# A decoder layer's expert phase: transposes in 64-row halves, rows turned one tile further ahead

## The chip, the cores and the metric

The kernel runs on one core of one Trainium2 chip. The time is the device time of the whole program in microseconds, the median of three runs. The profile is one further execution, recorded by the hardware profiler.

## The reference

One post-norm decoder layer on x of 128 sequences x 128 tokens x 256 features, all in fp32: causal self-attention (16 heads of 64), cross-attention (16 heads of 16, key mask), and two groups of 32 experts, each with top-2 routing. The change lies in the experts alone. For one group:

```python
order = jnp.argsort(flat_e)
tok = flat_t[order]
xs = x2[tok]
gate = lax.ragged_dot(xs, wg, group_sizes)
up = lax.ragged_dot(xs, wu, group_sizes)
ys = lax.ragged_dot(jax.nn.silu(gate) * up, wd, group_sizes)
ys = ys * flat_w[order][:, None]
return jnp.zeros_like(x2).at[tok].add(ys)
```

There are 16384 tokens, so 32768 rows in each group; an expert's weights are 256x128 (gate, up) and 128x256 (down).

## The kernel before, in words

The program has an attention phase (to about 3400 us) that also routes the tokens and scatters their rows, sorted by expert, to HBM (`xs_d`), and an expert phase. The change is in the expert phase (L1251 to L1532). It works through 576 tiles of 128 rows, each of one expert, 288 for each group; all weights stay in SBUF (`moe`), and TensorE finds the tile's expert by a word of a table that it reads once in four tiles (`find_weights`, L1381, the load on L1397).

Each engine runs its own queue of instructions in program order; semaphores order them among each other. All queues are written by the same loop over iterations n, in which an engine works on several tiles at different stages: `t.live(lag)` and `t.item(lag)` stand for tile n - lag. On TensorE one iteration is: transpose of tile n's rows (L1411, two of 128x128, from `xg` into the bank pair `XB`, one bank per tile in turn); gate and up of tile n-1 (L1419, two matmuls of 256 columns, each of which the chip runs as two passes); finding the weights; transpose of tile n-2's hidden activation h (L1430, one of 128x128 into `HB`); down product of tile n-3 (L1435, one matmul, two passes).

ScalarE copies the transposed rows (L1447) and the transposed h (L1451) from PSUM to SBUF and computes SiLU (L1455), in the order rows n, h of n-2, SiLU of n-1. VectorE multiplies by up (L1496), copies y (L1508) and combines finished rows of tokens; GpSimd writes y to HBM by token (L1366). SyncE loads rows into ten buffers ahead (L1331). TensorE waits for the rows' load, for ScalarE's copy of an earlier tile before it overwrites a bank, and for ScalarE's copies before it uses them.

A transpose on TensorE is a weight load of the data (here 128 columns wide) and a pass of the identity matrix over it. The attention phase uses other tilings of the array too: scores in 64-row halves (L779, pairs into two banks), cross scores in 32-row quarters (L792), and products in 32-column strips (L835, L851); all else works on 128x128.

Of the kernel before, what the change touches and what calls it, by code (L numbers as in the profile page):

```python
# [20 lines left out]
F32 = mybir.dt.float32  # L21
# [8 lines left out]
P = 128  # L30
D = 256
KC = D // P
# [62 lines left out]
def wait(eng, sem, value):  # L95

    if isinstance(value, int) and value <= 0:
        return
    eng.wait_ge(sem, value)
# [67 lines left out]
def decoder_layer(nc, xT, x, cT, mask, wq, wk, wv, wo, xwq, xbq, xwk, xbk, xwv, xbv, xwo, xbo,  # L167
# [4 lines left out]
    NT = NGRP * TILES  # L172
# [10 lines left out]
    keep = ExitStack()  # L183
    with keep:
        def tile(stack, name, shape, dt=F32):
            return stack.enter_context(nc.sbuf_tensor(name, shape, dt))
# [1 line left out]
        def sem(name):  # L188
            return keep.enter_context(nc.semaphore(name))

        banks = [keep.enter_context(nc.psum_tensor(f"bank{i}", [P, 512], F32)) for i in range(8)]


        ident = tile(keep, "ident", [P, P])
# [40 lines left out]
        with ExitStack() as one:  # L235
            def sb(name, shape, dt=F32):
                return tile(one, name, shape, dt)
# [66 lines left out]
            HALVES = (slice(0, P // 2), slice(P // 2, P))  # L304
# [946 lines left out]
        with ExitStack() as two:  # L1251
            def sb(name, shape, dt=F32):
# [6 lines left out]
            NQ, NX, NTO, NR, NS = 4, 10, 8, 4, 8  # L1259
# [14 lines left out]
            xg_s = [sb(f"xg{q}", [P, D + 2]) for q in range(NX)]  # L1274
            to = sb("to", [P, NTO], I32)
            xgT = [sb(f"xgT{q}", [P, KC, P]) for q in (0, 1)]
            gate_s = [sb(f"gate{q}", [P, HID]) for q in (0, 1)]
            h_s = [sb(f"h{q}", [P, HID]) for q in (0, 1)]
            hT_s = [sb(f"hT{q}", [P, P]) for q in (0, 1)]
# [1 line left out]
            stat, mv2 = sb("stat", [P, 6]), sb("mv2", [P, NR, 2])  # L1281
            ve, rstd = sb("ve", [P, NR]), sb("rstd", [P, NR])
            half1 = sb("half1", [P, 1])
            XB, GB, HB, YB = banks[0:2], banks[2:4], banks[4], banks[5:7]

            tabs_ready, pack_step, spare_ready, to_made = (
                sem(n) for n in ("tabs_ready", "pack_step", "spare_ready", "to_made"))
            xg_in = [sem(f"xg_in{q}") for q in range(NX)]
            xgt_made, xgt_in, gu_made, gate_in, h_in, ht_made, ht_in, y_made, y_in = (
                sem(n) for n in ("xgt_made", "xgt_in", "gu_made", "gate_in", "h_in", "ht_made", "ht_in", "y_made", "y_in"))  # L1290
# [27 lines left out]
            with nc.Block() as block:  # L1318
# [53 lines left out]
                @block.tensor  # L1372
                def _(pe):
                    pe.wait_ge(tabs_ready, 1)

                    word, next_word, at_place = (pe.alloc_register(n) for n in ("word", "next_word", "at_place"))
                    columns = [pe.alloc_register(f"column{q}") for q in range(NQ)]
                    loads = [pe.alloc_register(f"load{q}") for q in range(NQ)]
                    pe.reg_load(next_word, tabs[0:1, 0:1])

                    def find_weights(t, group):  # L1381

                        q = t.slot(0)
                        if t.p == 0:
                            pe.reg_mov(word, next_word)
                        pe.reg_alu(at_place, word, q * PLACE_BITS, ALU.logical_shift_right)
                        pe.reg_alu(at_place, at_place, 2 ** PLACE_BITS - 1, ALU.bitwise_and)
                        pe.reg_alu(columns[q], at_place, WCOL, ALU.mult)
                        pe.reg_alu(at_place, at_place, CHUNK.bit_length() - 1, ALU.logical_shift_right)
                        if group:  # L1390
                            pe.reg_alu(at_place, at_place, 4, ALU.add)
                        pe.reg_alu(at_place, at_place, (6, 7)[group], ALU.bitwise_and)
                        pe.reg_alu(at_place, at_place, (2, 5)[group], ALU.add)
                        pe.reg_alu(at_place, at_place, CHUNK_LOAD, ALU.mult)
                        pe.reg_alu(loads[q], at_place, 2 * CHUNK_LOAD, ALU.max)
                        if t.p == 2 and t.u + 1 < NT // PACK:
                            pe.reg_load(next_word, tabs[0:1, bass.ds(t.u + 1, 1)])  # L1397

                    def column(q):
                        return pe.snap(columns[q], min_val=0, max_val=(PLACES - 1) * WCOL)  # L1400

                    def iteration(t, n):

                        if t.live(1):
                            gate_up, load = column(t.slot(1)), pe.snap(loads[t.slot(1)], min_val=0, max_val=9 * CHUNK_LOAD)
                        if t.live(0):
                            q = t.slot(0)
                            pe.wait_ge(xg_in[n % NX], (n // NX + 1) * 16)
                            wait(pe, xgt_in, t.item(1))
                            for k in range(KC):  # L1410
                                last = nc.tensor.transpose(XB[q % 2][:, k * P:(k + 1) * P], xg_s[n % NX][:, k * P:(k + 1) * P], ident[:, :])  # L1411
                            last.then_inc(xgt_made, 1)
                        if t.live(1):
                            q = t.slot(1)
                            pe.wait_ge(moe_in, load)
                            pe.wait_ge(xgt_in, t.item(1) + 1)
                            wait(pe, h_in, t.item(2))
                            for k in range(KC):
                                last = nc.tensor.matmul(GB[q % 2][:, 0:2 * HID], xgT[q % 2][:, k, :],  # L1419
                                                        moe_cols[:, bass.ds(gate_up + k * 2 * HID, 2 * HID)], start=(k == 0), stop=(k == KC - 1))  # L1420
                            last.then_inc(gu_made, 1)
                        if t.live(3):
                            down = pe.snap(column(t.slot(3)) + KC * 2 * HID)
                        if t.live(0):
                            find_weights(t, int(n >= TILES))
                        if t.live(2):
                            q = t.slot(2)
                            pe.wait_ge(h_in, t.item(2) + 1)
                            wait(pe, ht_in, t.item(2))
                            nc.tensor.transpose(HB[:, 0:P], h_s[q % 2][:, :], ident[:, :]).then_inc(ht_made, 1)  # L1430
                        if t.live(3):
                            q = t.slot(3)
                            pe.wait_ge(ht_in, t.item(3) + 1)
                            wait(pe, y_in, t.item(4))
                            nc.tensor.matmul(YB[q % 2][:, 0:D], hT_s[q % 2][:, :], moe_cols[:, bass.ds(down, D)],  # L1435
                                             start=True, stop=True).then_inc(y_made, 1)

                    tiles(iteration)

                @block.scalar  # L1440
                def _(act):
                    def iteration(t, n):
                        if t.live(0):
                            q = t.slot(0)
                            act.wait_ge(xgt_made, t.item(0) + 1)
                            wait(act, gu_made, t.item(1))
                            nc.scalar.copy(xgT[q % 2][:, :, :].rearrange("p k t -> p (k t)"), XB[q % 2][:, 0:D]).then_inc(xgt_in, 1)  # L1447
                        if t.live(2):
                            q = t.slot(2)
                            act.wait_ge(ht_made, t.item(2) + 1)  # L1450
                            nc.scalar.copy(hT_s[q % 2][:, :], HB[:, 0:P]).then_inc(ht_in, 1)  # L1451
                        if t.live(1):
                            q = t.slot(1)
                            act.wait_ge(gu_made, t.item(1) + 1)
                            nc.scalar.activation(gate_s[q % 2][:, :], GB[q % 2][:, 0:HID], ACT.Silu).then_inc(gate_in, 1)  # L1455
                        now = combined(n)
                        if now:
                            g, b, k = now
                            wait(act, stored[k % NS], k // NS * 16)
                            act.dma_start(sums[k % NS][:, :], (x2_d, acc_d)[g][b * P:(b + 1) * P, :]).then_inc(sums_in[k % NS], 16)  # L1460
                            wait(act, sum_ready, k - NR + 1)
                            for q in range(NQ):
                                act.wait_ge(y_out[q], 16 * -(-(g * TILES + tiles_with(b) - q) // NQ))
                            act.dma_start(rows[:, k % NR, :, :].rearrange("p j d -> p (j d)"),
                                          y_of_token[b * P:(b + 1) * P, g * TOPK * D:(g + 1) * TOPK * D]).then_inc(rows_in[k % NR], 16)

                    tiles(iteration)
# [113 lines left out]
```

## Time and profile before

| what | value |
|---|---|
| median of 3 runs | 4448.16 us (4447.42 to 4455.27) |
| profiled execution | 4455.09 us |
| its span | 4453.3 us |
| TensorE busy over the span | 4345.7 us (98%) |
| TensorE weight loads | 3811.3 us (86%) |
| VectorE | 3593.6 us (81%) |
| ScalarE | 3260.3 us (73%) |
| GpSimd | 2715.9 us (61%) |

The busy share is over both phases. PE is TensorE's passes, PEld its weight loads, which run beside the passes; a pass's end is modelled, so the step between the starts of two passes says more than the duration of one. In the chain of work that ended last, followed back from the end, the four TensorE lines of the expert phase come first (L1419 10%, L1435 5%, L1411 3%, L1430 2% of the span).

### The profile page before, as it was taken

To read this page: it belongs to the slowest core of one execution; us is meant where nothing else is said; L and a number is where in the kernel's file an instruction comes from. 1 tells how busy PE (TensorE), PEld (TensorE's weight loads), DVE (VectorE), ACT (ScalarE), POOL (GpSimd) and SP (SyncE) were. 2 spreads that over 40 slices of the span, in tenths; PEclk is the share of its full clock that TensorE was granted. 3 is DMA by queue.
4 is the path that set the end of the run, shared out by engine and by line. 5 is a ranking of instruction groups with operands and counts; after the bars stand their busy time and mean duration, and the time that the engine had idled before them with its cause. 6 is when DMAs were issued, how large, how long until landed. Compare 5 with 4: busy or idle time off the path is not lost. (4 is left out here: it accounts for less than half of the span.)

```text
span 4453.3 us, 137987 instructions
## 1 busy us (share of the span) xinstructions
PE 4345.7 (98%) x42944; PEld 3811.3 (86%) x42944; DVE 3593.6 (81%) x18057; ACT 3260.3 (73%) x12741; POOL 2715.9 (61%) x3747
## 2 busy tenths in 40 slices
PE   8999999999999999999999999999995999999998
PEld 7888888989898989888988898999883778878886
DVE  4888888888888888888888888888885466658888
ACT  6888888888888888888888888888883444444444
POOL 3466566666666665666566656665665555557777
PEclk9999999999999999999999999999996999999999
DMA  5122212112212121122121212222115799988998
GB/s 171 57 68 67 69 63 69 66 63 72 69 66 69 65 68 66 65 72 68 66 70 65 67 66 67 71 68 71 63 62 172 219 342 338 311 276 288 310 310 292
DMA packets 477454, 552.60 MB, mean 124 GB/s; under 512 B 55633, under 2 KB 408145, under 8 KB 476241
## 3 DMA queue, kind: packets, MB, share of 16 engines
q1 hardware_dynamic: 350800, 296.21, 20.8%
q0 software_dynamic: 52224, 146.87, 8.7%
q10 hardware_dynamic: 73728, 100.70, 7.3%
q8 instruction: 376, 6.16, 0.6%
q14 instruction: 326, 2.66, 0.2%
HBM read 266.21 MB, written 277.35 MB: 122 GB/s over the span
## 5 line engine op out<-in xcount | busy, mean ns | idle before, releaser
L902 ACT ACTIVATE prob<-prob,negmax 128x128 f32<-128x128 f32 x2048 | 796.8, 392 | 258.3 <-DVE negmax L1038 258.3
L902 ACT ACTIVATE xprob<-xprob,xnegmax 128x128 f32<-128x128 f32 x2048 | 798.4, 399 | 3.6 <-DVE xnegmax L1038 3.6
L1366 POOL DMA_INDIRECT y_d<-y,to x576 | 562.9, 977 | 354.1 <-DVE y L1508 271.8
L1038 DVE CUSTOM_DVE_ANT_0 prob<-bank,causal 128x128 f32<-128x128 f32 x2048 | 453.8, 286 | 339.5 <-PE bank L792 322.6
L641 POOL DMA_INDIRECT xs_d<-xrow,place x512 | 551.8, 1078 | 139.2 <-issue 139.2
L1419 PE MATMUL bank<-moe,xgT 128*128 x2304 | 595.8, 381 | 1.3 <-issue 1.1
L604 POOL TENSOR_TENSOR rs<-spread_v,minus_half 128x1 f32<-128x1 f32 x256 | 170.9, 668 | 594.5 <-DVE spread_v L1112 591.7
L587 POOL CAST yTh<-yT 128x512 fp32r<-128x512 f32 x256 | 221.2, 864 | 461.3 <-ACT yT L938 461.3
L1038 DVE CUSTOM_DVE_ANT_0 xprob<-bank,xmask 128x128 f32<-128x128 f32 x2048 | 451.9, 287 | 0.5 <-PE bank L792 0.5
L1086 DVE TENSOR_TENSOR xprob<-xprob,xinv 128x512 f32<-128x512 f32 x512 | 438.0, 856 | 17.6
L690 PE MATMUL bank<-xT0h,wqkv 128*128 128x256 f32 x2048 | 436.3, 297 | 12.8 <-DVE wqkv L436 11.4
L690 PE MATMUL bank<-xT1h,wqkv 128*128 128x256 f32 x2048 | 435.5, 296 | 0.0
L1419 PEld LDWEIGHTS bank<-moe,xgT 128*128 128x128 f32 x2304 | 393.8, 191 | 34.1 <-issue 3.9
L902 ACT ACTIVATION_READ_ACCUMULATOR xprob<-xprob,xnegmax 128x1 f32 x2048 | 403.1, 197 | 0.0
L1447 ACT COPY xgT<-bank 128x256 f32<-128x256 f32 x576 | 214.5, 372 | 248.9 <-DMA y_d<-y,to 81.3
L902 ACT ACTIVATION_READ_ACCUMULATOR prob<-prob,negmax 128x1 f32 x2048 | 385.8, 188 | 0.0
L690 PEld LDWEIGHTS bank<-xT0h,wqkv 128*128 128x128 f32 x2048 | 333.3, 189 | 55.7 <-issue 40.8
L1075 DVE TENSOR_TENSOR prob<-prob,inv 128x512 f32<-128x512 f32 x512 | 358.2, 700 | 17.6
L690 PEld LDWEIGHTS bank<-xT1h,wqkv 128*128 128x128 f32 x2048 | 331.7, 188 | 43.2 <-issue 41.1
L1451 ACT COPY hT<-bank 128x128 f32<-128x128 f32 x576 | 152.9, 265 | 293.4 <-PE bank L1430 221.8
L1435 PE MATMUL bank<-moe,hT 128*128 x1152 | 359.0, 393 | 0.3
L589 POOL TENSOR_TENSOR yTl<-yT,yTh 128x512 fp32r<-128x512 f32 x256 | 328.7, 1284 | 21.0
(174 smaller groups left out, 13236.7 us busy)
## 6 DMA issues: line engine op xcount, KB each, us to landing
xg<-xs_d SPq DMA_DIRECT2D x576, 129.0 KB
xs_d<-blank SPq DMA_DIRECT2D x248, 272.0 KB
rows<-y_d ACTq DMA_DIRECT2D x256, 256.0 KB
xT_s<-xT SPq DMA_DIRECT2D x128, 128.0 KB, 2.7
cT<-cT SPq DMA_DIRECT2D x128, 128.0 KB, 2.1
x_s<-x SPq DMA_DIRECT2D x128, 128.0 KB
x_d<-x SPq DMA_DIRECT2D x128, 128.0 KB
sums<-x_d ACTq DMA_DIRECT2D x128, 128.0 KB
```

The source lines that it names most:

```text
L587: nc.gpsimd.tensor_copy(yT_p[0][:, c, :], yT[:, :, :]).then_inc(y_high, 1)
L589: nc.gpsimd.tensor_tensor(yT_p[1][:, c, :], yT[:, :, :], yT_p[0][:, c, :].bitcast(F32), ALU.subtract).then_inc(y_split, 1)
L641: nc.gpsimd.indirect_dma_start(xs_d[j // TOPK][:, :], bass.IndirectOffsetOnAxis(ap=place[p][:, j:j + 1].bitcast(U32), axis=0), xrow[p][:, ...
L690: last = nc.tensor.matmul(out_ap, lhs(a, k), rhs(b, k), start=(i == 0), stop=(i == len(todo) - 1))
L902: last = nc.scalar.activation(dst[:, h, :], dst[:, h, :], ACT.Exp, bias=src_bias[:, h:h + 1], scale=-1.0, accum_out=acc[:, h:h + 1])
L1038: last = nc.vector.tensor_tensor_reduce(dst[:, h, :], heads(h), bias[:, :], -1.0, float("inf"), ALU.add, ALU.min, least[:, h:h + 1])
L1075: nc.vector.tensor_tensor(prob[:, n % 2, h, :], prob[:, n % 2, h, :], spread(inv[:, h], 2, P), ALU.mult).then_inc(normed, 1)
L1086: nc.vector.tensor_tensor(xprob[:, x % 2, h, :], xprob[:, x % 2, h, :], spread(xinv[:, h], 2, P), ALU.mult).then_inc(xnormed, 1)
L1366: nc.gpsimd.indirect_dma_start(y_d[:, :], bass.IndirectOffsetOnAxis(ap=to[:, m % NTO:m % NTO + 1].bitcast(U32), axis=0), y_s[q][:, :], Non ...
L1419: last = nc.tensor.matmul(GB[q % 2][:, 0:2 * HID], xgT[q % 2][:, k, :], moe_cols[:, bass.ds(gate_up + k * 2 * HID, 2 * HID)], start=(k == ...
L1435: nc.tensor.matmul(YB[q % 2][:, 0:D], hT_s[q % 2][:, :], moe_cols[:, bass.ds(down, D)], start=True, stop=True).then_inc(y_made, 1)
L1447: nc.scalar.copy(xgT[q % 2][:, :, :].rearrange("p k t -> p (k t)"), XB[q % 2][:, 0:D]).then_inc(xgt_in, 1)
```

## The change

Rows and h are transposed in two halves of 64 rows. The halves lie in different row halves of the array and write into two banks of a pair: `XB` is now one pair of banks (banks 0 and 1) and `HB` another (2 and 3); gate/up and down keep two banks each in turn. A half's transpose loads 64 rows by 128 columns of data and passes a 64x64 identity over it. The rows' transposes move from the start of an iteration to behind the transposes of h, and take the rows of tile n+1 instead of n; the first iteration turns tile 0 ahead of all else. ScalarE's two copies read the halves from both banks. The bank tensors are declared in pairs, so their names change in all phases; the attention phase is otherwise as it was.

```diff
--- before.py
+++ after.py
@@ -188,7 +188,8 @@
         def sem(name):
             return keep.enter_context(nc.semaphore(name))
 
-        banks = [keep.enter_context(nc.psum_tensor(f"bank{i}", [P, 512], F32)) for i in range(8)]
+        bank_pairs = [keep.enter_context(nc.psum_tensor(f"banks{i}", [P, 2, 512], F32)) for i in range(4)]
+        banks = [bank_pairs[i // 2][:, i % 2, :] for i in range(8)]
 
 
         ident = tile(keep, "ident", [P, P])
@@ -1281,7 +1282,8 @@
             stat, mv2 = sb("stat", [P, 6]), sb("mv2", [P, NR, 2])
             ve, rstd = sb("ve", [P, NR]), sb("rstd", [P, NR])
             half1 = sb("half1", [P, 1])
-            XB, GB, HB, YB = banks[0:2], banks[2:4], banks[4], banks[5:7]
+            XB, HB, GB, YB = bank_pairs[0], bank_pairs[1], banks[4:6], banks[6:8]
+            HALVES = (slice(0, P // 2), slice(P // 2, P))
 
             tabs_ready, pack_step, spare_ready, to_made = (
                 sem(n) for n in ("tabs_ready", "pack_step", "spare_ready", "to_made"))
@@ -1399,17 +1401,24 @@
                     def column(q):
                         return pe.snap(columns[q], min_val=0, max_val=(PLACES - 1) * WCOL)
 
+                    def turn_rows(m):
+
+                        if m >= NT:
+                            return
+                        pe.wait_ge(xg_in[m % NX], (m // NX + 1) * 16)
+                        wait(pe, xgt_in, m)
+                        for k in range(KC):
+                            for side in (0, 1):
+                                last = nc.tensor.transpose(XB[:, side, k * P // 2:(k + 1) * P // 2], xg_s[m % NX][HALVES[side], k * P:(k + 1) * P],
+                                                           ident[HALVES[side], HALVES[side]])
+                        last.then_inc(xgt_made, 1)
+
                     def iteration(t, n):
 
+                        if n == 0:
+                            turn_rows(0)
                         if t.live(1):
                             gate_up, load = column(t.slot(1)), pe.snap(loads[t.slot(1)], min_val=0, max_val=9 * CHUNK_LOAD)
-                        if t.live(0):
-                            q = t.slot(0)
-                            pe.wait_ge(xg_in[n % NX], (n // NX + 1) * 16)
-                            wait(pe, xgt_in, t.item(1))
-                            for k in range(KC):
-                                last = nc.tensor.transpose(XB[q % 2][:, k * P:(k + 1) * P], xg_s[n % NX][:, k * P:(k + 1) * P], ident[:, :])
-                            last.then_inc(xgt_made, 1)
                         if t.live(1):
                             q = t.slot(1)
                             pe.wait_ge(moe_in, load)
@@ -1427,7 +1436,10 @@
                             q = t.slot(2)
                             pe.wait_ge(h_in, t.item(2) + 1)
                             wait(pe, ht_in, t.item(2))
-                            nc.tensor.transpose(HB[:, 0:P], h_s[q % 2][:, :], ident[:, :]).then_inc(ht_made, 1)
+                            for side in (0, 1):
+                                last = nc.tensor.transpose(HB[:, side, 0:P // 2], h_s[q % 2][HALVES[side], :], ident[HALVES[side], HALVES[side]])
+                            last.then_inc(ht_made, 1)
+                        turn_rows(n + 1)
                         if t.live(3):
                             q = t.slot(3)
                             pe.wait_ge(ht_in, t.item(3) + 1)
@@ -1444,11 +1456,11 @@
                             q = t.slot(0)
                             act.wait_ge(xgt_made, t.item(0) + 1)
                             wait(act, gu_made, t.item(1))
-                            nc.scalar.copy(xgT[q % 2][:, :, :].rearrange("p k t -> p (k t)"), XB[q % 2][:, 0:D]).then_inc(xgt_in, 1)
+                            nc.scalar.copy(xgT[q % 2][:, :, :].rearrange("p k (s t) -> p s k t", s=2), XB[:, :, 0:P].rearrange("p s (k t) -> p s k t", k=KC)).then_inc(xgt_in, 1)
                         if t.live(2):
                             q = t.slot(2)
                             act.wait_ge(ht_made, t.item(2) + 1)
-                            nc.scalar.copy(hT_s[q % 2][:, :], HB[:, 0:P]).then_inc(ht_in, 1)
+                            nc.scalar.copy(hT_s[q % 2][:, :].rearrange("p (s t) -> p s t", s=2), HB[:, :, 0:P // 2]).then_inc(ht_in, 1)
                         if t.live(1):
                             q = t.slot(1)
                             act.wait_ge(gu_made, t.item(1) + 1)
```

TensorE's queue in a tile of the middle of the phase, before: rows (L1411), gate/up (L1419), h (L1430), down (L1435); the ISA and register rows compute addresses of weights, and a pair of passes is one MATMUL row here.

```order
L1392 REGISTER_ALU
L1393 ISA
L1430 MATMUL bank<-ident,h 128x128 [waits ht_in,h_in]
L1435 ISA [waits y_in,ht_in]
L1435 MATMUL bank<-moe,hT 128x256
L1400 ISA
L1411 MATMUL bank<-ident,xg 128x128 [waits xgt_in,xg_in8]
L1411 MATMUL bank<-ident,xg 128x128
L1419 ISA [waits h_in,xgt_in,moe_in]
L1419 MATMUL bank<-moe,xgT 128x256
L1419 ISA
```

The same place after (rows are L1412, gate/up L1428, h L1440, down L1447): h and rows now stand together, each MATMUL of a 64-row half.

```order
L1394 REGISTER_ALU
L1395 ISA
L1440 MATMUL banks<-ident,h 128x64 [waits ht_in,h_in]
L1440 MATMUL banks<-ident,h 128x64
L1412 MATMUL banks<-ident,xg 128x64 [waits xgt_in,xg_in8]
L1412 MATMUL banks<-ident,xg 128x64 x3
L1447 ISA [waits y_in,ht_in]
L1447 MATMUL banks<-moe,hT 128x256
L1402 ISA
L1428 ISA [waits h_in,xgt_in,moe_in]
L1428 MATMUL banks<-moe,xgT 128x256
L1428 ISA
```

The rows' transposes moved from between down and gate/up to between h and down; one transpose of h became two, two of the rows became four, and the waits for ScalarE's copy and for the rows' load went with them.

## Rows read from the trace of the kernel before

**Rows 1.** Busy time of the engines in two stretches (attention phase, expert phase):

```profile
core 0: us, PE busy (x) PEld busy (x) DVE busy (x) ACT busy (x) POOL busy (x), PEclk, DMA share, GB/s
100.00:3300.00 3200.00, 3198.05 (x36074) 2877.56 (x36071) 2736.65 (x14599) 2660.45 (x10528) 1948.18 (x2839) 1.00 0.20 67
3446.70:4437.10 990.40, 977.69 (x5184) 792.59 (x5184) 701.25 (x2710) 468.35 (x1729) 636.80 (x694) 1.00 0.91 299
```

**Rows 2.** L1430 alone: stretch, length, PE busy (count), PEld busy (count), clock, DMA:

```profile
3600.00:4400.00 800.00, 129.40 (x468) 65.61 (x467) 1.00 0.94 310
```

**Rows 3.** TensorE in time (start us, us, engine, line, operation, tile, count, [idle before]):

```profile
4005.17 0.38 PE L1411 MATMUL bank<-ident,xg 128*128 128x128 f32 x2
4005.39 1.03 PE L1419 MATMUL bank<-moe,xgT 128*128 x4
4006.25 0.27 PE L1430 MATMUL bank<-ident,h 128*128 128x128 f32 x1
4006.36 0.60 PE L1435 MATMUL bank<-moe,hT 128*128 x2
4006.79 0.38 PE L1411 MATMUL bank<-ident,xg 128*128 128x128 f32 x2
...
4008.42 0.27 PE L1411 MATMUL bank<-ident,xg 128*128 128x128 f32 x1
```

**Rows 4.** All engines in order of time: TensorE in one fourth tile:

```profile
4001.71 0.38 PE L1411 MATMUL bank<-ident,xg 128*128 128x128 f32 x2
...
4002.70 0.14 PEld L1430 LDWEIGHTS bank<-ident,h 128*128 128x128 f32 x1
...
4003.00 0.30 PEld L1435 LDWEIGHTS bank<-moe,hT 128*128 128x128 f32 x2 [0.16 <-issue]
...
4003.54 0.38 PE L1411 MATMUL bank<-ident,xg 128*128 128x128 f32 x2
```

**Rows 5.** TensorE in order of time, changes of tiling in the attention phase:

```profile
2004.44 1.03 PE L683 MATMUL bank<-xwv_s,cT 128*128 128x256 f32 x4
2005.40 1.08 PE L835 MATMUL bank<-probT,v 128*32 128x128 f32 x32
...
2006.85 1.16 PE L779 MATMUL bank<-kT,qT 64*128 64x128 f32 x16
2007.94 0.71 PE L792 MATMUL bank<-xkD,xqT 32*128 32x256 f32 x8
2008.58 0.38 PE L690 MATMUL bank<-xT1h,wqkv 128*128 128x256 f32 x1
2008.81 0.28 PE L690 MATMUL bank<-xT1l,wqkv 128*128 128x256 f32 x1
2008.92 0.40 PE L690 MATMUL bank<-xT1h,wqkv 128*128 128x256 f32 x2
```

**Rows 6.** TensorE in order of time, first scores, behind 128-row passes:

```profile
34.31 0.62 PE L690 MATMUL bank<-wqkv,xT0h 128*128 128x512 f32 x2
34.78 0.40 PE L690 MATMUL bank<-wqkv,xT0l 128*128 128x512 f32 x1
35.10 1.16 PE L779 MATMUL bank<-kT,qT 64*128 64x128 f32 x16
```

**Rows 7.** TensorE in order of time, transposes behind a change and a wait:

```profile
3316.06 0.44 PE L733 MATMUL bank<-ident,x 128*128 128x128 f32 x2
...
3744.19 0.44 PE L1411 MATMUL bank<-ident,xg 128*128 128x128 f32 x2 [1.76 <-DMA xg<-xs_d]
```

**Rows 8.** All engines in order of time: ScalarE behind the transpose of h:

```profile
4001.17 0.27 PE L1430 MATMUL bank<-ident,h 128*128 128x128 f32 x1
...
4001.64 0.28 ACT L1455 ACTIVATE gate<-bank 128x128 f32<-128x128 f32 x1
...
4002.13 0.37 ACT L1447 COPY xgT<-bank 128x256 f32<-128x256 f32 x1 [0.21 <-issue]
```

**Rows 9.** Waits in the expert phase (engine, line, released by: us, times, longest):

```profile
ACT xgT L1447 <- DMA y_d<-y,to: 77.4, 135, 1.7
```

## The prediction

> **What bounds the kernel now.** I read the busy table by stretch first. In the expert phase, from the first transpose of rows at 3446.7 us to the last pass of the down product at about 4437 us, TensorE is busy 977.69 of 990.40 us at a granted clock of 1.00, the higher of its two levels (2.4 GHz), VectorE 701.25, ScalarE 468.35 [rows 1]. So the phase is TensorE's, and the reader should look for what TensorE does in one tile. The count of hidden-activation transposes gives the mean: 468 tiles in 800 us, 1.709 us each [rows 2]. The timeline gives an undisturbed tile: from one row transpose to the one two tiles on 3.25 us, so 1.625 a tile (1.63 below), with no idle bracket [rows 3]. In it two row transposes take 0.22 (4005.17 to 4005.39), the four gate/up passes 0.86 (0.215 each), the transpose of h 0.11, the two down passes 0.43. The three transposes, which are all that the change touches, are 0.33 of 1.63 us.
>
> The difference between the mean and the undisturbed tile, 1.709 - 1.63 = 0.08 us, is 46 us over 576 tiles. Its largest visible part is every fourth tile, in which TensorE's queue reads the next word of its table: there the load for the h transpose starts at 4002.70 and that for the down product at 4003.00 after 0.16 us of "issue", and the tile takes 1.83 us (4001.71 to 4003.54) [rows 4]. 144 such tiles at 0.20 us are 29 us.
>
> **The change part by part.** The h transpose and the two row transposes of 128x128 become three pairs of 64-row transposes: 3 weight loads and 3 passes become 6 and 6, each load still 128 columns wide, each pass 64 columns instead of 128. The two halves of a pair sit in different row halves of the array and different banks, so they can run at once. They stand together between gate/up and down; so the array goes from 128-row work to 64-row work and back once per tile. The trace of before has no such alternation in this phase, but the attention phase has all its parts.
>
> 1. *Passes.* A pair of 64-row passes: the 16 score passes (8 pairs, 128 columns each) take 1.09 us from 2006.85 to 2007.94 [rows 5]; one after the other, at the 0.11 of a 128-column transpose [rows 3], they would take 1.76. Pairs therefore do run together. With half the columns I take half of 0.11, plus a few ns of issue: 0.058 a pair. Bounds: 0.055 (half), and 0.11 (if the weight load, which is not halved, sets the step). I choose near the lower end because of the load price in 3. Three pairs: 0.174 instead of 0.33, a gain of 0.155.
>
> 2. *Draining at a change of tiling.* Four 256-column passes start at 2004.44; at 0.215 the next instruction is due at 2005.30 and comes at 2005.40: 0.10 lost, with no wait named [rows 5]. In the first scores, which follow 128-row passes directly, the last of those starts at 34.78 and the 64-row work at 35.10, 0.32 later, against 0.235 a pass before (34.31 to 34.78 for two): 0.09 lost [rows 6]. I take 0.095 on entering and 0.09 on leaving.
>
> 3. *The first weight load behind a change.* In an undisturbed stream loads lie under the passes before. Behind a change they don't: the first 128-row pass after the 32-row scores takes from 2008.58 to 2008.81, 0.23, where the next takes 0.11 [rows 5]: 0.11 lost for a load of ordinary fp32 weights. The score pairs agree: 1.09 less 8 x 0.11 leaves 0.21, which is one such load and one drain. So do the 32-row scores: 0.64 less two passes of 0.215 leaves 0.21. For a transpose the exposed load is smaller: the two transposes that follow the 32-row scores take 0.44 in place of 0.38, and so do the two row transposes that follow a wait for rows [rows 7, 3], so 0.055. On entering, the h transposes pay 0.055; on leaving, the down product pays about 0.105.
>
> Sum of the stretch between gate/up and down: 0.095 + 0.055 + 0.174 + 0.09 + 0.105 = 0.52 us instead of 0.33: +0.19 to +0.195 a tile, 1.82 us in place of 1.63, on the engine that bounds the phase. 576 tiles: +112 us.
>
> The Trainium skill, "TensorEngine Tiling (Array Packing)", section Tiling Modes under Key Properties, says that a change of tiling mode, unlike a change of tile, drains TensorE. The rows above agree, with 0.09 to 0.10 a change, and add that the next load is then uncovered too. The packing rule of the Trainium skill, "TensorE: Matmul & The Clock Gate", Part 3, promises concurrency of row tiles; by it alone the tile would lose 0.155 us, which is the faster rival below.
>
> 4. *What is given back.* The queue's lateness in every fourth tile finds room. There the h load came 0.12 after its place beside the last gate/up pass (4002.70 against 4001.71 + 0.22 + 3 x 0.215 = 4002.58); it is now due 0.31 after it. The down load came at 0.42; it is now due at 0.31 + 0.055 + 2 x 0.058 + 0.15 = 0.63, with four extra loads, four passes and the rows' waits issued ahead of it. I take the 29 us as gone and keep the other 17 of the 46. Bounds: nothing given back (+112) and all 46 (+66).
>
> 5. *Costed at nothing.* The rows are turned one tile further ahead, from one pair of banks instead of two in turn, so a turn waits until ScalarE has copied the rows before. Behind that wait on TensorE stand the down product and all that follows. The copy is 0.37 us; it stands behind the SiLU, which starts 0.47 us after the h transpose (4001.17 to 4001.64) and lasts 0.28, and so can end about 1.1 us after that transpose at the earliest [rows 8]; the next turn comes 1.9 us after it. The cover is 0.8 us. Where ScalarE is held by a row write to HBM (135 waits, 77.4 us, longest 1.7 [rows 9]) the cover can fail; at 0.3 us for the tenth of the tiles with the longest waits that is 17 us, inside the range, and the longer tile leaves these writes more time. The copy reads the same 256 elements from two banks: same duration. The phase before has the same instructions in the same banks. The rows' loads from HBM are needed one tile earlier out of ten buffers; the one 1.76 us wait shown [rows 7] is of a kind that a slower TensorE makes rarer.
>
> Total: +112 - 29 = +83, rounded to +82. The profiled execution took 4455.09 us (span 4453.3 and 1.8 outside it), which becomes 4537; the median of the runs is 6.9 us lower, 4448.16, and becomes **4530 us**.
>
> **Rivals.**
> - *Faster: 64-row transposes enter and leave without drain or bare load.* For it: the two row halves are disjoint, and the 64-column passes are short. Against it: every one of the changes in [rows 5, 6] pays, between three tilings and into transposes as well. Tile 1.63 - 0.155 = 1.475, so -89 us, 4359; with TensorE's queue late in every fourth tile as now, part of that stays lost. In a middle form the drains are paid and the loads are pulled under them: 0.185 - 0.155 = +0.03 a tile, 17 us, which the 29 us given back outweigh: 4436 to 4448.
> - *Slower than forecast: the step of a pair is the step of a whole transpose*, because the 128-column load sets it (0.11), or because two transposes of a pair don't overlap (2 x 0.055). Then three pairs are 0.33, nothing is saved, and both changes are paid in full: the tile is 1.63 + 0.345 or a little more, +199 us, less 29: 4618. For it: loads are not halved. The Trainium skill, "TensorE: Matmul & The Clock Gate", section LDWEIGHTS, gives a load by its columns alone, 128 / 1.2 = 107 ns, which is this case. Against it: the 0.055 of an exposed transpose load [rows 7] against 0.11 of an ordinary one [rows 5].
> - *ScalarE's copy becomes the wait of every tile* (single pair of banks). It decides once the copy ends later than 1.9 us after the h transpose; with 1.1 us at best and 135 delayed copies it stays at some 17 us: 4547.
> - *The granted clock falls* in the drains. Against it: the attention phase changes its tiling again and again [rows 5] and its mean is 1.00 [rows 1]. Not priced.
>
> **How the numbers follow.** Forecast with its own range (give-back between 0 and 46 us, drains and loads each a few ns either way): 0.74, 4500 to 4570, ScalarE's waits included. Pairs at the step of whole transposes: 0.15, 4618. Loads hidden under drains: 0.05, at or just under the time before. No price at all: 0.06. The range reaches down to the forecast's low end and up over the slow case, 4495 to 4625; 0.11 is left out below it. A difference under 0.2% (9 us) can't be told from none. Faster: 0.08 (the free case and half of the middle one); same: 0.02; slower: 0.90.
>
> **What would show it.** In the profile after: an undisturbed tile near 1.82 us in the timeline; between the last gate/up pass and the first h load about 0.31 us; the three pairs within some 0.12 us from the first pass to the last; the first down pass taking about 0.32 instead of 0.215; TensorE's idle brackets with no engine named; the fourth tile no longer longer than the others. A step of 0.11 between pairs is the slow rival; gate/up to h at 0.215 is the fast one. Wrong altogether if row transposes show idle time released by ScalarE's copy, or if the attention phase changes length.

## The result, and the profile after

The changed kernel is slower: 4542.88 us, the median of four runs (4536.73 to 4547.23), against 4447.79 (4446.58 to 4455.27) for the kernel before beside it; the ratio is 1.0205, with an interval of 1.0192 to 1.0218 (the quotient of the two medians is 1.0214). The forecast was 4530. The profiled execution took 4547.23 us, with a span of 4545.4, 92.1 more than before.

First the two stretches of [rows 1], read in the same view (columns as there):

```profile
100.00:3300.00 3200.00, 3198.07 (x36080) 2878.33 (x36077) 2736.70 (x14597) 2660.27 (x10528) 1945.87 (x2839) 1.00 0.20 67
3448.20:4528.90 1080.70, 1066.55 (x6912) 771.36 (x6912) 708.77 (x2710) 437.98 (x1729) 629.95 (x694) 1.00 0.86 274
```

The attention phase is what it was: 3198.07 us of TensorE busy in 3200, against 3198.05. The expert phase, from the first row transpose to the last down pass, takes 1080.7 us instead of 990.4, TensorE as busy as before (98.7% of it) and at the same granted clock of 1.00. Its passes are 6912 instead of 5184, 12 a tile instead of 9. So the +90 us are TensorE's, in this phase; the start comes 1.5 us later. The count of h transposes, the answer to [rows 2], gives the mean tile:

```profile
3600.00:4400.00 800.00, 118.44 (x858) 60.27 (x858) 1.00 0.89 284
```

858 halves are 429 tiles in 800 us, 1.865 us each against 1.709. An undisturbed tile (no idle time of TensorE in it but what every tile has) is read from TensorE's timeline, as in [rows 3] (rows are L1412, gate/up L1428, h L1440, down L1447):

```profile
4001.09 1.03 PE L1428 MATMUL banks<-moe,xgT 128*128 x4
4002.04 0.28 PE L1440 MATMUL banks<-ident,h 64*128 64x64 f32 x2
4002.16 0.29 PE L1412 MATMUL banks<-ident,xg 64*128 64x64 f32 x4
4002.37 0.70 PE L1447 MATMUL banks<-moe,hT 128*128 x2
4002.91 1.03 PE L1428 MATMUL banks<-moe,xgT 128*128 x4
```

From 4001.09 to 4002.91 it is 1.82 us. Of the four gate/up passes three take a step of 0.216 and the last 0.31, so h starts 0.95 after the first, not 0.86. The rows' halves come 0.12 after h's, the down product 0.21 after the rows', and gate/up 0.54 after that instead of 0.43.

Taken over the 575 steps from one start of gate/up to the next, the median tile is 1.824 us (1.628 before), 0.196 more, which is 112.7 us. What the tiles lie above that median ("lost" below; between two kinds of passes, what the steps from one start to the other exceed their own median) sums to 26.5 us in after and 49.0 before. 112.7 less 22.5 is the +90.

### The profile page after: what moved, and what is told of

The parts are those of the page before. It is cut to its first block and busy times, and to the rows that moved or that the text cites. A ratio compares the mean times of both kernels' runs of the same rounds, so it can differ in the third digit from the quotient of the medians.

```text
span 4545.4 us, 141446 instructions
## 1 busy us (share of the span) xinstructions
PE 4434.7 (98%) x44672; PEld 3790.8 (83%) x44672; DVE 3601.9 (79%) x18057; ACT 3230.4 (71%) x12741; POOL 2707.7 (60%) x3747
## 5 line engine op out<-in xcount | busy, mean ns | idle before, releaser
L1039 DVE CUSTOM_DVE_ANT_0 prob<-banks,causal 128x128 f32<-128x128 f32 x2048 | 453.7, 286 | 339.1 <-PE banks L793 322.2
L1428 PE MATMUL banks<-moe,xgT 128*128 x2304 | 594.8, 381 | 0.0
L1428 PEld LDWEIGHTS banks<-moe,xgT 128*128 128x128 f32 x2304 | 439.9, 191 | 59.8
L1039 DVE CUSTOM_DVE_ANT_0 xprob<-banks,xmask 128x128 f32<-128x128 f32 x2048 | 451.4, 286 | 0.2 <-PE banks L793 0.2
L691 PE MATMUL banks<-xT0h,wqkv 128*128 128x256 f32 x2048 | 436.4, 297 | 13.4 <-DVE wqkv L437 12.0
L691 PE MATMUL banks<-xT1h,wqkv 128*128 128x256 f32 x2048 | 435.6, 296 | 0.0
L1447 PE MATMUL banks<-moe,hT 128*128 x1152 | 403.4, 432 | 0.0
L691 PEld LDWEIGHTS banks<-xT0h,wqkv 128*128 128x128 f32 x2048 | 333.5, 190 | 56.2 <-issue 40.7
L691 PEld LDWEIGHTS banks<-xT1h,wqkv 128*128 128x128 f32 x2048 | 332.0, 189 | 43.1 <-issue 41.0
L1459 ACT COPY xgT<-banks 128x256 f32<-128x256 f32 x576 | 216.8, 376 | 177.4 <-DMA y_d<-y,to 137.9
```

The costliest lines, as they stand in the source:

```text
L691: last = nc.tensor.matmul(out_ap, lhs(a, k), rhs(b, k), start=(i == 0), stop=(i == len(todo) - 1))
L1039: last = nc.vector.tensor_tensor_reduce(dst[:, h, :], heads(h), bias[:, :], -1.0, float("inf"), ALU.add, ALU.min, least[:, h:h + 1])
L1459: nc.scalar.copy(xgT[q % 2][:, :, :].rearrange("p k (s t) -> p s k t", s=2), XB[:, :, 0:P].rearrange("p s (k t) -> p s k t", k=KC)).then_i ...
```

## The experiments

"Tile" below is the median from one start of gate/up to the next, unless a mean is named. Code is cut to the lines that matter; `...` marks what is left out.

### 1. The new order with whole transposes

```diff
-    for side in (0, 1):
-        last = nc.tensor.transpose(XB[:, side, k * P // 2:...], xg_s[m % NX][HALVES[side], ...], ident[HALVES[side], HALVES[side]])
+    last = nc.tensor.transpose(XB[:, m % 2, k * P:(k + 1) * P], xg_s[m % NX][:, k * P:(k + 1) * P], ident[:, :])
```

(The same for h; ScalarE's copies read one bank, and the turn waits for the copy of one tile earlier, since the rows have two banks in turn again.)

> The new order (rows one tile further ahead, behind h), but whole 128x128 transposes, rows again in two banks in turn. Theory (the price is paid at the changes of tiling, 0.35 us a tile, against 0.155 saved): no change of tiling, so an undisturbed tile takes 1.63 us as before; rows now stand between h and down, which gives TensorE's queue 0.22 us more in every fourth tile, so that some or all of the 29 us lost there come back: 4420 to 4448 us. Rival (the move itself costs: rows further ahead, ScalarE's copies later): near 4540, with waits of TensorE on ScalarE. Rival (six short transposes cost more than three whole ones): 4448.

4445.17 us, ratio 0.9996 (0.9986 to 1.0005). TensorE's timeline (rows L1411, gate/up L1426, h L1437, down L1443):

```profile
4001.72 1.03 PE L1426 MATMUL banks<-moe,xgT 128*128 x4
4002.58 0.27 PE L1437 MATMUL banks<-ident,h 128*128 128x128 f32 x1
4002.69 0.38 PE L1411 MATMUL banks<-ident,xg 128*128 128x128 f32 x2
4002.91 0.60 PE L1443 MATMUL banks<-moe,hT 128*128 x2
4003.34 1.03 PE L1426 MATMUL banks<-moe,xgT 128*128 x4
```

The same work in the new order takes 1.62 us, with steps of 0.86, 0.11, 0.22 and 0.43 as in [rows 3]. The expected gain in the fourth tiles hardly came (their median is 1.73 where before has 1.77). The move costs nothing and gives nothing that can be measured; the whole loss belongs to the halves and to the single pair of banks that they need.

### 2. The halves at the old places

```diff
-                        if n == 0:
-                            turn_rows(0)
                         if t.live(1):
                             gate_up, load = column(t.slot(1)), ...
+                        turn_rows(n)
...
-                        turn_rows(n + 1)
```

> 64-row halves as in the changed kernel, but in the old order: rows ahead of gate/up, h ahead of down, so two entries and two exits of the tiling per tile. Theory (price per change of tiling): rows 0.095 + 0.055 + 2 x 0.059 + 0.09 + 0.105 = 0.46 instead of 0.22, h 0.40 instead of 0.11, so a tile of 1.63 + 0.54 = 2.17 us, 576 x 0.54 = 311, less up to 40 given back: 4720 to 4760 us. Rival (the price is in the halves themselves, their number of instructions): as the changed kernel, 4543. Rival (the price is in the order): 4448.

4717.18 us in the one run of this kernel, just under the expected range; the tile is 2.165 against a forecast of 2.17 by the price of one more entry and exit. TensorE's timeline (rows L1412, gate/up L1427, h L1439, down L1445):

```profile
4000.81 0.34 PE L1412 MATMUL banks<-ident,xg 64*128 64x64 f32 x4
4001.07 1.13 PE L1427 MATMUL banks<-moe,xgT 128*128 x4
4002.13 0.28 PE L1439 MATMUL banks<-ident,h 64*128 64x64 f32 x2
4002.34 0.70 PE L1445 MATMUL banks<-moe,hT 128*128 x2
4002.97 0.34 PE L1412 MATMUL banks<-ident,xg 64*128 64x64 f32 x4
```

Four changes a tile instead of two. The tile is 2.16 us (4000.81 to 4002.97), 0.34 above that of after for one entry and exit more. From gate/up to h it is 1.06 where after has 0.95, since the first gate/up pass now follows a change too. The mean is 2.168: only 1.9 us are lost above the median, so that all but 2 of before's 49 us come back where at most 40 were expected. At this length of tile the queues are no longer late, though the order is the old one.

### 3. One half of each pair

```diff
-                            for side in (0, 1):
+                            for side in (0,):
```

(for the rows and for h; the other half of each is left out, so this kernel does not compute the layer)

> The changed kernel with only the first half of each pair transposed; the second half of rows and of h is left out (stale numbers stand in its bank), all changes of tiling remain. Theory (the two halves of a pair overlap fully, the second costs its issue, some 3 ns): tile 1.82 us less 0.01, total 4530 to 4545. Rival (the halves run one after the other, or each instruction has its price): three halves less, 0.03 to 0.06 each, tile 1.65 to 1.74, 4440 to 4495.

4533.09 us, one run; tile 1.820 against 1.824 with both halves. TensorE's timeline:

```profile
4001.92 1.03 PE L1428 MATMUL banks<-moe,xgT 128*128 x4
4002.88 0.27 PE L1440 MATMUL banks<-ident,h 64*128 64x64 f32 x1
4002.99 0.28 PE L1412 MATMUL banks<-ident,xg 64*128 64x64 f32 x2
4003.20 0.70 PE L1447 MATMUL banks<-moe,hT 128*128 x2
```

h to rows 0.11, rows to down 0.21: the steps of after, with half the passes; the rows' two remaining transposes, both in the same row half of the array, follow each other at 0.062. So the second half of a pair runs wholly beside the first, and what the stretch costs beyond 0.059 a pair is the two changes. In after the starts of the two halves of a pair lie 0.003 us apart.

### 4. Fewer changes: rows of two tiles, then of four, at once

```diff
-                        if m >= NT:
+                        if m >= NT or m % 2:
                             return
                         wait(pe, xgt_in, m)
+                        for j in range(m, m + 2):
...
-                        last.then_inc(xgt_made, 1)
+                        last.then_inc(xgt_made, 2)
```

h is turned whole again. For four tiles each 2 becomes a 4.

> Whole transposes of h; rows in 64-row halves, for two tiles at once in every second iteration, so one entry and one exit of the tiling per two tiles. Theory (price per change of tiling): per two tiles 0.095 + 0.055 + 4 x 0.059 + 0.09 + 0.105 = 0.58 instead of 0.44, so 0.07 us a tile: mean undisturbed tile 1.70, 576 x 0.07 = +40, less 0 to 29 given back in every fourth tile: 4460 to 4488 us. Rival (price per half): rows have two thirds of the halves, so two thirds of the loss, +0.13 a tile: 4495 to 4523.

4505.73 us, ratio 1.0127 (1.0110 to 1.0144). TensorE's timeline (rows L1414, gate/up L1430, h L1441, down L1447):

```profile
4002.11 1.03 PE L1430 MATMUL banks<-moe,xgT 128*128 x4
...
4003.18 0.46 PE L1414 MATMUL banks<-ident,xg 64*128 64x64 f32 x8
4003.57 0.70 PE L1447 MATMUL banks<-moe,hT 128*128 x2
4004.11 1.03 PE L1430 MATMUL banks<-moe,xgT 128*128 x4
...
4005.51 0.81 PE L1430 MATMUL banks<-moe,xgT 128*128 x3
```

The price holds: 2.00 us for the tile with the burst and 1.40 for the one without, 3.40 for two; the medians are 1.992 and 1.407. Against two tiles of 1.628 that is +0.144, and with four pairs' gain of 0.051 each (0.11 less 0.059) the entry and exit cost 0.348. But the mean is 1.80, not 1.70, and the time is the rival's. TensorE's largest wait between 3580 and 4430 us says why (engine, line, released by: us, times, longest):

```profile
PEld banks L1414 <- ACT xgT L1459: 81.2, 218, 1.6
```

The burst needs both tiles' columns of the bank pair free, and ScalarE copies the second tile's rows in the very iteration that ends with the next burst. The mean lies 0.10 above the 1.70 of undisturbed tiles, some 60 us in all. 26 of them are lost right ahead of the bursts, where this wait (81 us with what lies beside passes) is TensorE's largest, and 11 between h and down. The tile being short again, the fourth tiles are late again too: by place in four the medians are 2.09, 1.57, 2.00 and 1.41, so the tile whose queue reads the word and the next lose 0.1 and 0.16.

> Whole transposes of h; rows in 64-row halves for four tiles at once in every fourth iteration: one entry and one exit of the tiling per four tiles. Theory (price per change of tiling, 0.345 us for an entry and an exit, 0.05 saved per row transpose): undisturbed four tiles 4 x 1.628 - 0.88 + 0.095 + 0.055 + 8 x 0.059 + 0.09 + 0.105 = 6.45, 1.61 each, under the kernel before; the wait for ScalarE's last copy ahead of each of 144 bursts adds 0.2 to 0.4 us a burst: total 4440 to 4490. Rival (price per half): as with two tiles at once, undisturbed tile 1.70 or more.

4522.73 us, one run: missed, and more than with two. TensorE's timeline:

```profile
4002.88 1.03 PE L1430 MATMUL banks<-moe,xgT 128*128 x4
...
4004.29 1.03 PE L1430 MATMUL banks<-moe,xgT 128*128 x4
...
4005.69 1.03 PE L1430 MATMUL banks<-moe,xgT 128*128 x4
...
4007.40 1.03 PE L1430 MATMUL banks<-moe,xgT 128*128 x4
...
4009.65 1.03 PE L1430 MATMUL banks<-moe,xgT 128*128 x4
```

Two short tiles take 1.41 and 1.40, but the third 1.71 (4005.69 to 4007.40), and the tile with the burst of 16 takes 2.25. The waits:

```profile
PEld banks L1441 <- DVE h L1508: 41.0, 94, 0.9
PEld banks L1414 <- ACT xgT L1459: 35.7, 108, 1.5
PEld banks L1414 <- DMA xg<-xs_d: 27.1, 37, 5.2
```

Eight pairs at once need four tiles' rows in SBUF and four copies by ScalarE, one after the other: TensorE waits for the rows' loads (27 us), for the copies (36) and for h (41). The 1.61 us a tile that the price gives for such a burst, (4 x 1.628 + 0.348 - 8 x 0.051) / 4, was not seen.

### 5. Why ScalarE's copy is late: y's landing, or its own queue

In after 16.6 us are lost between h and rows, the term that the prediction costed at nothing (1.9 of them in one wait for a row load from HBM). The profile names "DMA y_d<-y,to" as the releaser of the copy that is late. Ahead of that copy on ScalarE's queue stands the read of the tokens' y rows (rows<-y_d), and two causes fit: it waits for y to land, or its issue takes long. If it is the landing, reading two iterations later removes the loss:

```diff
-            FIRST, COMBINE, FINAL, STORE = E + 10, 4, 9, 16
+            FIRST, COMBINE, FINAL, STORE = E + 12, 4, 9, 16
```

> The changed kernel; finished rows are read back and combined two iterations later (FIRST from E + 10 to E + 12), so ScalarE, which issues these reads, waits less for y to have landed, and its copies of rows come earlier. Theory (the 16 us that TensorE loses ahead of the row transposes in the changed kernel are ScalarE held by those landings): that loss falls under 6 us, the undisturbed tile stays at 1.824, total 4527 to 4537 against 4543. Rival (the copy is late by its own chain behind h and SiLU): the loss stays, 4543.

4546.62 us, ratio 1.0223 (1.0208 to 1.0239). Its waits, the answer to [rows 9]:

```profile
ACT xgT L1459 <- DMA y_d<-y,to: 122.4, 220, 1.6
...
PE banks L1412 <- ACT xgT L1459: 7.3, 12, 0.9
...
PEld banks L1412 <- DMA xg<-xs_d: 2.7, 1, 2.7
```

122 us with this releaser instead of 130 in after, and 15.6 us lost between h and rows instead of 16.6 (12.9 instead of 14.7 without the one row load in each): the forecast was missed, and y's landing is not it. The issues themselves are as long with y two iterations older: 17 us above their median together, the longest 1.55, against 18 and 1.94 in after. The other cause is the issue itself, so that DMA was given to SyncE's queue, with the waits ahead of it:

```diff
+                        now = combined(n - 9)
+                        if now:
+                            ...
+                            sp.dma_start(rows[:, k % NR, :, :]..., y_of_token[...]).then_inc(rows_in[k % NR], 16)
...
-                            act.dma_start(rows[:, k % NR, :, :]..., y_of_token[...]).then_inc(rows_in[k % NR], 16)
```

> The changed kernel; the gathers of finished rows (rows<-y_d) are issued by SyncE's queue instead of ScalarE's. Theory (the 16 us that TensorE loses ahead of the row transposes are ScalarE's own issue of these gathers, 0.33 us as a rule and up to 1.94, in front of its copy of rows): that loss falls under 4 us, undisturbed tile 1.824, total 4526 to 4534 against 4543. Rival (ScalarE is held by its chain behind h and SiLU alone): the loss stays near 16, 4543.

4575.06 us, ratio 1.0285 (1.0269 to 1.0300). The loss between h and rows is gone (0.2 us), and the copy's wait of 130 us is gone from the list of waits (what is left is 1.1 us in 4 waits, with no engine named). That confirms the cause, though the time lost elsewhere gives the copy some room as well; that the issue stands ahead of a late copy is seen directly in the trace of after, shown further on. The forecast for the whole was missed: 44.6 us are now lost between gate/up and h, where after loses 5.5. The waits:

```profile
DVE sums L1518 <- DMA rows<-y_d: 80.2, 84, 3.5
PEld banks L1448 <- DVE h L1511: 56.0, 76, 2.9
PE banks L1448 <- DVE h L1511: 27.1, 39, 2.5
```

SyncE issues the rows later (2.4 us in the median, behind its own loads of rows), VectorE's combining waits for them, and h, queued behind that on VectorE, comes late to TensorE. The place on ScalarE's queue costs some 15 us; this one costs more. A place further ahead in SyncE's queue, or a later combining beside it, was not tried.

### 6. Can the kernel before be helped by the same things

Its lateness in every fourth tile was tried by reading the table word behind the down product:

```diff
-                        if t.p == 2 and t.u + 1 < NT // PACK:
-                            pe.reg_load(next_word, tabs[0:1, bass.ds(t.u + 1, 1)])
...
+                        if t.live(0) and t.p == 2 and t.u + 1 < NT // PACK:
+                            pe.reg_load(next_word, tabs[0:1, bass.ds(t.u + 1, 1)])
```

> The kernel before; the read of the table word that TensorE's queue makes in every fourth tile stands behind the down product instead of between gate/up and h. Theory (the 29 us lost in fourth tiles, which the changed kernel gets back, are that read delaying the issue of h and down): fourth tiles fall from 1.77 (median) to under 1.70, total 4420 to 4440 against 4448. Rival (TensorE's queue has no time to spare anywhere, the loss only moves to another place): fourth tiles as long as before, 4448. Undisturbed tile 1.63 in both.

4447.86 us, ratio 0.9997 (0.9988 to 1.0006): the rival. The medians of the tile by its place in four were 1.628, 1.628, 1.77, 1.628 before and are 1.628, 1.628, 1.628, 1.73 here. The lateness moves with the read and stays.

All of it together, the order of 1, this read and the later combining:

> Whole transposes in the new order (rows one tile further ahead, behind h), the table word read behind the down product, finished rows combined two iterations later. Theory (with no change of tiling, what is left over the undisturbed tile are these two latenesses): undisturbed tile 1.625, mean under 1.67, total 4415 to 4435. Rival (the lateness of TensorE's queue is its own length per tile and only moves): 4440 to 4448.

4446.29 us, ratio 0.9992 (0.9983 to 1.0001): again the rival. The undisturbed tile is 1.625, the mean 1.701; before 1.713. What an edit took away at one place came back at another.

The read of y's rows on SyncE's queue (edit as in 5), in the kernel before and on top of the kernel of the last run:

> The kernel before; the gathers of finished rows are issued by SyncE's queue instead of ScalarE's. Theory: the copy has more than a tile's cover there, but h waits behind the same issue, and TensorE loses 13 us between gate/up and h, of which half or more comes back: 4435 to 4444 against 4448, undisturbed tile 1.63. Rival (that loss is TensorE's own queue in fourth tiles): no difference, 4448.

4522.57 us, ratio 1.0168 (1.0154 to 1.0181).

> Whole transposes in the new order, table word read behind the down product, combining two iterations later, and the gathers of finished rows issued by SyncE's queue. Theory (what the order, the table and the landings did not free is ScalarE's issue of the gathers): mean tile from 1.70 to under 1.68, total 4425 to 4440. Rival (something else paces the mean tile at 1.70): 4443 to 4450.

4527.92 us, ratio 1.0167 (1.0153 to 1.0181). Both forecasts failed for the reason of 5. The waits of the first (h is L1438, of VectorE L1499):

```profile
DVE sums L1506 <- DMA rows<-y_d: 103.2, 96, 4.4
...
PEld bank L1438 <- DVE h L1499: 86.5, 92, 4.1
PE bank L1438 <- DVE h L1499: 51.2, 58, 3.7
```

78.5 us are lost between gate/up and h, 91.7 in the other; before loses 14.8 there. No version came out below the kernel before by more than can be measured.

## Why the prediction was right

The sign and the mechanism were right, step by step, and the time was 13 us short. That it came so near is in part luck, since two of the losses that the sum kept or left out (4 and 5) moved against each other.

1. *Passes.* A pair steps 0.059 (0.058 forecast); experiment 3 shows that a pair costs what one half does. The rival of pairs at 0.11 falls.
2. *Drains.* On entering 0.310 - 0.216 = 0.094 (0.095); on leaving 0.152 from the last pair to the down product, less 0.059, 0.093 (0.09). The attention phase pays what it did in [rows 5], 2005.23 to 2006.19 with four passes in it, again 0.96:

```profile
2005.23 1.03 PE L684 MATMUL banks<-xwv_s,cT 128*128 128x256 f32 x4
2006.19 1.08 PE L836 MATMUL banks<-probT,v 128*32 128x128 f32 x32
```

The Trainium skill, "TensorEngine Tiling (Array Packing)", section Tiling Modes, states this drain without a figure; the trace agrees.

3. *Bare loads* (weight loads that no pass covers). h to rows 0.109, of which 0.059 is the pair's step: 0.050 (0.055). First down pass 0.320 against 0.219: 0.101 (0.105). Drains, loads and passes add up to a tile of 1.824 (1.82), so +112.7 us (+112). Experiments 2 and 4 give the price of one entry and exit by themselves: 0.34 and 0.348. The free case and the middle one of the rivals fall with it. The Trainium skill, "TensorE: Matmul & The Clock Gate", section LDWEIGHTS, gives a load by its columns, by its formula an estimated 107 ns for 128. The down product's bare load agrees; ahead of the transposes only half as much is uncovered, and in experiment 3 transposes with loads of 128 columns follow each other at 0.062, so there the measurement decides.

4. *Given back.* The fourth tiles came back whole: medians by place 1.824, 1.823, 1.825, 1.823, where some 31 us lay before (29 forecast). The first run of experiment 6 corrects the reason a little: the lateness belongs to reading the word at all and goes where the read goes. The new order alone does not free it (experiment 1), the old order with a longer tile does (experiment 2): so it is the longer tile that makes the room, as far as these two runs tell. The other 18 us of before's 49 shrank to 10, where the sum kept 17.

5. *Costed at nothing: the term that was mis-sized.* The prediction gave ScalarE's copy a cover of 0.8 us, read from a tile without a DMA issue, and named 17 us if it failed. It failed, for 12 to 15 us, and one row load was 1.9 us late; so after kept 26.5 us above its median tile instead of 17. The condition that the prediction gave, ScalarE held by a row write to HBM, was a misreading of [rows 9], as experiment 5 shows. The waits of after:

```profile
PEld banks L1440 <- issue: 169.0, 505, 0.7
ACT xgT L1459 <- DMA y_d<-y,to: 130.3, 225, 2.1
...
PE banks L1412 <- ACT xgT L1459: 9.1, 15, 1.2
...
PEld banks L1412 <- DMA xg<-xs_d: 1.9, 1, 1.9
```

The first row is the forecast's idle time with no engine named, 0.33 before each h load. The second is 130 us in 225 waits where [rows 9] had 77 in 135, and 15 tiles in which the row transposes then wait up to 1.2 us for the copy: not a tenth of the tiles by 0.3, as the bound was built, but few and long. The prediction had named idle time of the row transposes released by ScalarE's copy as a sign of being wrong altogether. That sign came, and was drawn too sharply: the prediction's own bound for the same wait, 17 us, lay inside its range, and the tile's price is not touched by it. How it comes to that is seen in all engines' order of time; first a usual tile in which tokens are combined (ACTq is ScalarE's queue issuing a DMA):

```profile
4002.91 0.33 ACTq L1476 DMA_DIRECT2D rows<-y_d  x1
...
4003.33 0.37 ACT L1459 COPY xgT<-banks 128x256 f32<-128x256 f32 x1 [0.52 <-DMA y_d<-y,to]
...
4003.98 0.29 PE L1412 MATMUL banks<-ident,xg 64*128 64x64 f32 x4
```

The issue of rows<-y_d takes 0.33, from 4002.91; the copy of the rows follows, 4003.33 to 4003.70, and the turn that needs the banks comes at 3.98. The cover is 0.28 us here (4003.70 to 4003.98), not 0.8. And a late one:

```profile
4411.14 1.67 ACTq L1476 DMA_DIRECT2D rows<-y_d  x1
...
4412.17 0.28 PE L1440 MATMUL banks<-ident,h 64*128 64x64 f32 x2
...
4412.90 0.37 ACT L1459 COPY xgT<-banks 128x256 f32<-128x256 f32 x1 [1.86 <-DMA y_d<-y,to]
...
4413.42 0.34 PE L1412 MATMUL banks<-ident,xg 64*128 64x64 f32 x4 [0.97 <-ACT xgT L1459]
```

The issue takes 1.67 us, 4411.14 to 4412.81; the copy starts only at 4412.90; h is turned at 4412.17, and the row transposes, due at 4412.28, start at 4413.42. The 256 issues of this read have a median of 0.33 us, but the longest takes 1.94, and together they exceed the median by 18 us. In 16 tiles the row transposes come 0.41 to 1.39 us late behind the copy, 12.2 us in all, and in each of them the copy follows directly on an issue of 0.89 us or more. Experiment 5 shows that this, and not y's landing, is the cause; why an issue is sometimes long stays open. In before such issues are long too (longest 1.5, 12.8 us above the median), and in experiment 1 (longest 1.9), but with two banks in turn TensorE goes on: no wait of the row transposes for the copy is on the list of either.

Of the 10 us between 4537 and the 4547.23 of the profiled execution, 6.5 are the smaller give-back (22.5 for 29), 1 each the steady tile and a rounding, and 2 the start and what lies outside the tiles. The other 3 are the median, which lies 4.4 us below after's profiled execution, not 6.9 as before.

What stays open is why the kernels without halves, before and those of experiment 1 and the first two runs of 6, keep a mean near 1.70 against 1.625 undisturbed, wherever the single latenesses lie. A kernel that batches the rows and h of several tiles was not tried.

## What to carry to other kernels

Price a change of array tiling from the trace as an entry and an exit together, two drains and two bare weight loads (loads that no pass covers), and set it against what all the work between them gains: here 0.34 us against 0.051 a transpose, which needs some seven transposes a visit to the other tiling where this kernel has three. Making the visits rarer moved the cost here to the engines that fill and empty the batch (experiment 4). A DMA that an engine issues is time in that engine's queue, so where two banks in turn become one, read the cover in the tiles where the copying engine issues DMAs, and by the longest issue, not the usual one.

## What the runs showed of the hardware that was not expected

- The issue of one DMA (rows<-y_d) held ScalarE's queue for 0.33 us as a rule and for up to 1.94; issued two iterations later (up to 1.55) or from SyncE's queue (up to 1.81) it was no steadier. With its waits moved to SyncE's queue, behind the loads of rows, the kernel before lost 78.5 us instead of 14.8 between gate/up and h (ratio 1.0168).
- The bare load ahead of a transpose cost 0.050 us, that ahead of an ordinary fp32 pass 0.101, both 128 columns wide; 64-row transposes in one row half, each with such a load, stepped 0.062.
- Halves in two row halves of the array started 0.003 us apart, and dropping one half of every pair changed the tile by 0.004.
- What TensorE's tiles lay above their median in all, mostly for late queues, was 49.0 us at a tile of 1.63 us, 26.5 at 1.82 (16.6 of it new, ahead of the row transposes) and 1.9 at 2.17.
